# A fused attention and sparse-FFN kernel: the attention's output projection as three fp16 products instead of one fp32 product

## The reference

```
a = x
q, k, v = x@Wq, x@Wk, x@Wv          # 16 heads of 32
q, k = rotary(q), rotary(k)
attn = lightning_attn(q, k, v)      # linear attention in chunks of 128 tokens, a state carried from chunk to chunk
attn = attn * rsqrt(mean(attn^2) + 1e-5) * rms_w
attention_out = attn @ Wo           # <- the product that the change rewrites
z   = layernorm(x) @ ternary(W_syn).T + b_syn      # 2048 values per token
h   = z where z is among the top 204 of its token and positive, else 0
y   = h @ ternary(W_out).T + b_out
out = x-side terms + attention_out + layernorm(y-side)*gamma + beta
```

## Time and profile before

| what | value |
|---|---|
| median of 3 runs | 1044.32 us (1043.78 to 1046.3) |
| the profiled execution, its own time | 1045.96 us |
| its span, first to last instruction | 1044.0 us |
| mean granted TensorE clock | 0.973 |
| busy: PE, DVE, POOL, ACT | 971.1, 760.7, 694.9, 560.8 us |
| busy, PE, from 157.4 to 951.9 us | 794.5 of 794.5 us |

### The profile page before, as it was taken

The page is one execution under the profiler, slowest core; times in us unless marked ns, Lnnn a source line. Parts: engine busy times, 40 slices in busy tenths (PEclk is TensorE's granted clock), DMA queues, the critical chain, the costliest instruction groups (busy, mean ns, idle before and its releaser), DMA issues.

```text
span 1044.0 us, 18566 instructions
## 1 busy us (share of the span) xinstructions
PE 971.1 (93%) x6608; PEld 493.5 (47%) x6608; DVE 760.7 (73%) x2153; ACT 560.8 (54%) x715; POOL 694.9 (67%) x617
## 2 busy tenths in 40 slices
PE   1767799999999999999999999999999999999875
PEld 0333455554555555554555555554555555554432
DVE  2577767777877777777877777777877777776762
ACT  3877664654454665654455655654455655654421
POOL 1334777777778777777778777777777777777522
PEclk9978899999999999999999999999999999999976
DMA  9785756546455456545654555455554455555322
GB/s 295 258 201 91 145 88 112 101 92 112 100 103 96 83 96 112 97 97 111 97 107 78 96 101 111 92 101 111 93 111 89 81 104 110 89 106 101 72 51 60
DMA packets 328782, 113.65 MB, mean 109 GB/s; under 512 B 314736, under 2 KB 314992, under 8 KB 327792
## 3 DMA queue, kind: packets, MB, share of 16 engines
q1 hardware_dynamic: 326576, 108.25, 53.5%
q10 hardware_dynamic: 2112, 4.19, 1.3%
HBM read 25.38 MB, written 8.39 MB: 32 GB/s over the span
## 4 chain that ended last, share of the span: by engine, by line
PE 84%; DVE 1%; DMA 1%; issue 0%; POOL 0%; ACT 0%; SPq 0%; POOLq 0%; DVEq 0%
PE proj L735 42%; PE p_ffn L828 22%; PE p_wo L864 10%; PE p_av L803 3%; PE sbank L794 3%; PE p_av L849 2%; PE sbank L743 1%; PE sbank L885 1%; DMA area<-hl 1%; DVE area L1136 0%; PE sbank L897 0%; ACT hl L475 0%; PE p_wo L814 0%; POOL c L636 0%; SPq L299 0%
## 5 line engine op out<-in xcount | busy, mean ns | idle before, releaser
L735 PE MATMUL proj<-wqkv,xT 128*128 128x512 f16 x1152 | 257.6, 383 | 0.7 <-DVE wqkv L967 0.4
L735 PE MATMUL proj<-wsynT,xT 128*128 128x512 f16 x1024 | 246.2, 384 | 1.4 <-DVE area L1022 0.9
L828 PE MATMUL p_ffn<-woutT,area 128*128 128x512 f16 x1024 | 235.6, 385 | 10.9 <-DMA area<-hl 10.9
L735 PEld LDWEIGHTS proj<-wqkv,xT 128*128 128x128 f16 x1152 | 113.2, 99 | 131.7 <-issue 4.0
L468 ACT ACTIVATE Pr<-area,c 128x2048 f16<-128x2048 f32 x32 | 64.1, 2003 | 199.0 <-DVE c L1130 193.4
L828 PEld LDWEIGHTS p_ffn<-woutT,area 128*128 128x128 f16 x1024 | 101.9, 104 | 121.6 <-DMA area<-hl 11.1
L735 PEld LDWEIGHTS proj<-wsynT,xT 128*128 128x128 f16 x1024 | 93.2, 99 | 126.1 <-issue 35.0
L1022 DVE SCALAR_TENSOR_TENSOR area<-proj,c,gb 128x512 f32<-128x512 f32 x128 | 95.3, 745 | 42.8 <-PE proj L735 40.0
L631 POOL TENSOR_TENSOR hl<-area,hl 128x2048 f16<-128x2048 f32 x30 | 122.4, 4079 | 4.3 <-ACT hl L475 4.3
L864 PE MATMUL p_wo<-wo,pair_a 128*128 128x512 f32 x256 | 118.7, 607 | 0.0
L550 POOL TENSOR_TENSOR xhl<-xn,xhl 128x512 f16<-128x512 f32 x32 | 78.3, 2448 | 53.9 <-ACT xhl L397 53.9
(11 more groups left out here) (176 smaller groups left out, 1459.2 us busy)
## 6 DMA issues: line engine op xcount, KB each, us to landing
xr<-in_L_attn_x_dram SPq DMA_DIRECT2D x32, 256.0 KB, 3.2
out_dram<-pair_b SPq DMA_DIRECT2D x32, 256.0 KB, 2.1
area<-in_L_ffn_W_out_dram SPq DMA_DIRECT2D x3, 1024.0 KB, 6.0
woutT<-in_L_ffn_W_syn_dram ACTq DMA_DIRECT2D x2, 1024.0 KB, 13.2
area<-in_L_ffn_W_syn_dram ACTq DMA_DIRECT2D x2, 1024.0 KB, 17.7
woutT<-in_L_ffn_W_out_dram SPq DMA_DIRECT2D x2, 1024.0 KB, 6.5
area<-in_L_attn_Wq_dram SPq DMA_DIRECT2D x1, 1024.0 KB, 6.6
area<-in_L_attn_Wk_dram SPq DMA_DIRECT2D x1, 1024.0 KB, 9.7
```

The costliest lines, as they stand in the source:

```text
L735: last = nc.tensor.matmul(bank, xT[:, b.par, k, :], w, start=m == 0, stop=m == len(pairs) - 1)
L828: last = nc.tensor.matmul(p_ffn, hT[:, k, :], woutT[:, k % NB, :], start=k == 0, stop=k == 2 * NB - 1)
```

## The change

The Wo product becomes three fp16 products accumulated in one bank: high x high, high x low, low x high; twelve passes. The operands need a scale. Wo is multiplied by `rms_w`, its largest row sum is found as for the other weights, and it is scaled and split in the prologue. The attention output is multiplied, per token, by the power of two in `rstdR` (its exponent bits) times 256; the rest of `rstdR` (its mantissa) and the scale of Wo are put on at L1083. Since `aT` holds a token in a column, the powers have to be spread over the partitions: DVE puts them on a diagonal in bf16, and PE multiplies a tile of ones by it. The new names are `step_up`, `mant`, `diag`, `att_factor`, `ahl` (the halves).

The core of the diff:

```diff
-        wo = sb("wo", [P, KB, E], F32)
+        wo = sb("wo", [P, 2, KB, E], F16)
+        wo_in = masked.rearrange("p (b n) -> p b n", b=KB)
@@ SP, prologue
                 sp.wait_ge(S["syn_loaded3"], 16)
+                load_wo()
                 load(out_in[0], wt[:, 0, :], "out_loaded0")
                 load(dmask, t_dmask, "dmask_loaded")
-                load_wo()
@@ ACT, prologue, after qkv_out(second, 1)
+                act.wait_ge(S["wo_factor"], 1)
+                nc.scalar.activation(wo[:, 0], wo_in, ACT.Copy, scale=pc[:, 58:59]).then_inc(S["wo_high"], 1)
@@ ACT, step, between the second count (L483) and normalised(a)
+                wait(act, "an_ready", u, 1, 1)
+                wait(act, "wo_done", u, 1, 0)
+                nc.scalar.activation(ahl[:, 0], aT, ACT.Copy).then_inc(S["ah_ready"], 1)
@@ POOL, step, between the low half of h (L631) and low_half(a) (L550)
+                    wait(pool, "ah_ready", u, 1, 1)
+                    nc.gpsimd.tensor_tensor(ahl[:, 1], aT, ahl[:, 0], ALU.subtract).then_inc(S["al_ready"], 1)
@@ PE, prologue
                 projection(second, 1)
+                row_flipped(4)
+                row_spread(4)
                 projection(second, 2)
@@ PE, failures()
-                    nc.tensor.matmul(p_wo[:, 0:1], ones, fail, start=True, stop=True)
+                    nc.tensor.matmul(p_wo[0:1, 0:1], fail, ones[:, 0:1], start=True, stop=True)
@@ PE, step, after projection(b, 0)
+                    wait(pe, "diag_ready", u, 1, 1)
+                    nc.tensor.matmul(p_wo[:, P:2 * P], ones16, diag, start=True, stop=True)
@@ PE, step, the product
-                    wait(pe, "aT_ready", u, 1, 1)
-                    wait(pe, "fail_count", u, 1, 1)
-                    for g in range(HG):
-                        last = nc.tensor.matmul(p_wo, aT[:, g, :], wo[:, g, :], start=g == 0, stop=g == HG - 1)
+                    wait(pe, "ah_ready", u, 1, 1)
+                    terms = [(l, w, g) for l, w in ((0, 0), (0, 1), (1, 0)) for g in range(HG)]
+                    for m, (l, w, g) in enumerate(terms):
+                        if l and g == 0:
+                            wait(pe, "al_ready", u, 1, 1)
+                        last = nc.tensor.matmul(p_wo, ahl[:, l, g, :], wo[:, w, g, :], ...)
@@ DVE, prologue, after the bias sums, before syn_weights()
+                dve.wait_ge(S["wo_loaded"], 2 * 16)
+                for k in range(KB):
+                    last = nc.vector.tensor_scalar(wo_in[:, k, :], wo_in[:, k, :], rmsw[:, k:k + 1], None, ALU.mult)
+                last.then_inc(S["wo_scaled"], 1)
+                dve.wait_ge(S["wo_scaled"], 1)
+                nc.vector.reduce_sum(pc[:, 57:58], wo_in.rearrange("p b n -> p (b n)"), AX.X,
+                                     apply_absolute_value=True).then_inc(S["wo_abs"], 1)
+                row_topped(4)
+                dve.wait_ge(S["row_all"], 5)
+                then(nc.vector.tensor_scalar(pc[:, 59:60], p_ffn[:, 0:1], 1e-30, None, ALU.max))
+                pow2(pc[:, 60:61], pc[:, 59:60])
+                then(nc.vector.reciprocal(pc[:, 58:59], pc[:, 60:61]))
+                then(nc.vector.tensor_scalar(wo_back, pc[:, 60:61], 1.0 / (AS * WS), None, ALU.mult))
+                nc.vector.tensor_scalar(pc[:, 58:59], pc[:, 58:59], WS, None, ALU.mult).then_inc(S["wo_factor"], 1)
@@ DVE, prologue's end
+                nc.vector.scalar_tensor_tensor(wo[:, 1], wo_in, pc[:, 58:59], wo[:, 0], ALU.mult, ALU.subtract)
@@ DVE, step: factors(u), between the next guess (L1130) and masked (L1136)
+                    wait(dve, "rstdR_ready", u, 1, 1)
+                    nc.vector.tensor_scalar(step_up.bitcast(I32), rstdR.bitcast(I32), 0x7F800000, ...)
+                    nc.vector.tensor_scalar(mant.bitcast(I32), rstdR.bitcast(I32), 0x007FFFFF, 0x3F800000, ...)
+                    nc.vector.tensor_scalar(diag, ident, step_up, None, ALU.mult).then_inc(S["diag_ready"], 1)
+                    nc.vector.tensor_scalar(att_factor, mant, wo_back, None, ALU.mult)
@@ DVE, step: attention_normalised(u), after y and its statistics (L1166), before L1170
+                    wait(dve, "factors_spread", u, 1, 1)
+                    wait(dve, "aT_ready", u, 1, 1)
+                    spread = p_wo[:, P:2 * P].unsqueeze(1).to_broadcast([P, HG, P])
+                    nc.vector.scalar_tensor_tensor(aT, spread, AS, aT, ALU.mult, ALU.mult).then_inc(S["an_ready"], 1)
```

More of the change, by code:

```diff
@@ L37 @@
 WS = 2.0 ** 14
+AS = 256.0
 QS = 32.0
@@ L483, in step @@
                     nc.scalar.activation(unused, z[:, t.par, :], ACT.Sign, bias=nt1, accum_out=s2).then_inc(S["sum2"], 1)
+                if u:
+                    attention_high(u)
                 if a:
@@ L1058, in prologue @@
                                                ALU.add).then_inc(S["guess_ready"], 1)
-                dve.wait_ge(S["wo_loaded"], 2 * 16)
-                for k in range(KB):
-                    last = nc.vector.tensor_scalar(wo[:, k, :], wo[:, k, :], rmsw[:, k:k + 1], None, ALU.mult)
-                last.then_inc(S["wo_scaled"], 1)
+                dve.wait_ge(S["wo_high"], 1)
+                dve.wait_ge(S["wo_factor"], 1)
+                nc.vector.scalar_tensor_tensor(wo[:, 1], wo_in, pc[:, 58:59], wo[:, 0], ALU.mult,
+                                               ALU.subtract).then_inc(S["wo_low"], 1)
             def step(dve, i, p):
@@ L1081, in attention_added, with factors, attention_normalised @@
                     wait(dve, "beta_added", u, 1, 1)
+                    wait(dve, "factor_step", u, 3, 3)
+                    nc.vector.scalar_tensor_tensor(slot(xr, u), p_wo, att_factor, slot(xr, u), ALU.mult,
+                                                   ALU.add).then_inc(S["att_added"], 1)
+                def factors(u):
                     wait(dve, "rstdR_ready", u, 1, 1)
[L1083 to L1084 removed]
+                    nc.vector.tensor_scalar(step_up.bitcast(I32), rstdR.bitcast(I32), 0x7F800000, None,
+                                            ALU.bitwise_and).then_inc(S["factor_step"], 1)
+                    nc.vector.tensor_scalar(mant.bitcast(I32), rstdR.bitcast(I32), 0x007FFFFF, 0x3F800000, ALU.bitwise_and,
+                                            ALU.bitwise_or).then_inc(S["factor_step"], 1)
+                    wait(dve, "factor_step", u, 3, 1)
+                    nc.vector.tensor_scalar(diag, ident, step_up, None, ALU.mult).then_inc(S["diag_ready"], 1)
+                    wait(dve, "factor_step", u, 3, 2)
+                    nc.vector.tensor_scalar(att_factor, mant, wo_back, None, ALU.mult).then_inc(S["factor_step"], 1)
+                def attention_normalised(u):
+                    wait(dve, "factors_spread", u, 1, 1)
+                    wait(dve, "aT_ready", u, 1, 1)
+                    spread = p_wo[:, P:2 * P].unsqueeze(1).to_broadcast([P, HG, P])
+                    nc.vector.scalar_tensor_tensor(aT, spread, AS, aT, ALU.mult, ALU.mult).then_inc(S["an_ready"], 1)
                 def segments(k):
@@ L1166, in step @@
                     nc.vector.bn_stats(st6[:, 1, :], y).then_inc(S["yst"], 1)
+                if u:
+                    attention_normalised(u)
                 if t:
```

59 lines of the change are left out of this document (40 added, 19 removed).

## The result

The changed kernel took 1065.34 us (median of 4 runs, 1063.01 to 1068.48), and the kernel before 1044.05 beside it (4 runs, 1043.77 to 1046.3): a ratio of 1.0201, with a 95% interval from 1.0171 to 1.0231. It is slower by about 2%, and outside the predicted range (1026 to 1052). The profiled execution took 1065.79 us with a span of 1064.0, which is 20.0 more than before; its mean granted clock is 0.966 (0.973 before).

The account below looks back on a forecast made before the run. The prediction took TensorE's unbroken run of 29 steps of 29.43 us as the bound. Prologue +3.2, steps -9.6 and end +2.4 gave -4.0 us: 1040.0, or 1040.3 on the median, range 1026 to 1052.

Parts of the forecast that it names:

- The spreading product: PE, each step: one added bf16 pass of 128 columns, put at 0.08 us.
- The four operations of `factors`: DVE, ahead of `masked`: three one-column operations and a 128x128 one, put at 0.42 us, bounds 0.3 and 0.9.
- hold: DVE's L1186 (L1267 after the change) kept back by POOL's new low half, 0.95 us, bounds 0.5 and 1.2.
- The power for `rD`: POOL's L636, behind L550: 0.95 us late, with everything behind it on POOL.
- The wait for PE ahead of the first z chunk: DVE's 1.14 us idle time in each step, forecast to be gone.
- The end: Behind 981.39 us, where PE is not the bound: 2.4 us added, bounds 1 and 3.5.
- PE's own step: PE's work per step, forecast as 29.43 - 0.90 - 0.05 + 0.08 = 28.56 us.
- rival 4: `factors` on DVE's loop take 0.9 instead of 0.42, second count 0.5 later, step 29.6, kernel 1055 us; chance 0.15.
- What is late next: POOL's lateness followed to probabilities and sums of squares: loop 29.05, step taken as 29.1 us, 9.6 off over 29 steps.
- the term of 3.2 us: The prologue and second step, up to 127.87 us: 3.2 us added.
- first piece: Prologue: Wo lands at 39, scaling takes 1.89, PE waits 1.2 us; syn sums 2.2 us later, bounds 0.8 and 5.
- second piece: Second step: ACT's `attention_high` ahead of the signs that the last W_out transposes wait for, 0.55 us more.

Follow-up runs that it names:

- one more POOL operation: The kernel before with a 128x512 subtraction of constants added on POOL in each step, where the low half would go: 1045.61 us, 1.0004.
- POOL order run: The changed kernel with POOL's low halves of q and k ahead of the output sum, which waits for DVE's failure flag: 1047.85 us, 1.0017.
- late operation in the kernel before: The kernel before plus a 128x512 POOL subtraction per step that also waits for ACT's normalised x: 1049.61 us, 1.0031.

## Why the prediction was wrong

**What was right.** The row of L864 became 2.59 us of L904, as worked out. The spreading product takes 0.06 us of PE's step (0.08 predicted). The four operations of `factors` fill 0.50 us, from 620.35 to L1215 at 620.85 (0.42). POOL's operation goes first and L1267 takes 3.19 us (3.3), a hold of 0.84 (0.95). The power for `rD` is 1.05 us later behind the count (0.95). The wait for PE ahead of the first z chunk is gone. Ahead of L937 PE's weight load waits 0.68 us a step for POOL's sums of squares and PE itself 0.19, which lie side by side and don't add up (about 0.5 predicted); the piece of the chain is 0.38 us, where it was 0.12 (0.34). The end took 2.1 us more (2.4). The failure count did not get cheaper: 0.12 as before, 0.05 predicted off, and the half of the W_out product behind it takes 3.56 us in the chains of four of the kernels above, where it took 3.48. Why was not tried. With this PE's own step is 29.43 - 0.90 + 0.06 + 0.08 = 28.67 (28.56).

The size of the hold came out better than its reasoning. I scaled 0.23 us of an operation of 0.40 by the columns. What three rows have in common is another rule: DVE loses what is left of POOL's operation less 0.2 us. It lost 0.84 of 1.04 here, 0.22 of 0.43 beside the one more POOL operation, and 0.23 of 0.42 in the earlier trace rows.

One size was off without deciding anything. From the count read to `masked` it takes 2.52 us in the median step, where it took 1.49: besides `factors`, the branch lets DVE go on 0.42 us later (1.51 behind the read, 1.09 before). What the branch does there I did not test. `masked` itself takes 2.34 in every step, where it took 2.54 to 2.57 in 20 of 32, so its end comes 0.8 later. ACT hides most of it, as predicted, though not all: the second guess step L1254 comes 10.63 us behind the read, 10.44 before. So 0.19 arrive where I had 0.05, far from the 0.5 of rival 4.

**What failed in the steady part** is the step "What is late next", which gave 29.05 and 29.1 us for a step that measured 29.63. I followed POOL's 0.95 us of lateness by two ways, to the probabilities and to the sums of squares, and stopped there. A third way goes on over POOL's last operation, the low halves of q and k, to the end of DVE's top-k. I had said that POOL's work and two-operand DVE work add up, and applied it to L1186 only. The kernel before had the rows for it: L578 ends at 600.63, the selection starts at 600.68. The DVE loop, 28.9 in the prediction, plus 0.77 for the held flag, plus the 0.14 more of `factors` and less the 0.11 by which the hold was shorter, is 29.7, and 29.63 was measured; this sum was made afterwards and takes the flag's price for every step, though in half of them it was the selection, and those steps were longer (29.85 against 29.52). The POOL order run shows this cause alone, in size (0.67 us a step, 19.4 us over 29 steps), and the late operation in the kernel before shows it from the other side. And neither hold is dear alone: 28.96 with that of L1267, 28.84 with those of the top-k, 29.63 with both kinds.

With the meeting gone the step is 28.96, against 29.1 predicted. That part of the argument, a POOL–PE loop somewhat longer than PE's step, was right in its mechanism: moving the sums of squares took the wait away, and the step fell to 28.85. But it holds the step only 0.11 us above what is left without it, not the 0.54 between 28.56 and 29.1.

**What failed in the start** is the term of 3.2 us, of which 12.0 were measured. Its first piece (+2.2 for the syn sums, 6.4 measured) had Wo landing too late, at 39, and took 1.89 us for its scaling from a row with only 0.40 us of POOL work beside it; it took 4.85. The wait of PE that came of it, put at 1.2 us, was 3.91 (and 5.2 or 5.3 in the five other kernels with this prologue), and it cost a second time: the 12 passes behind it ran at a granted clock of 0.53 and took 2.36 us more. With 1.25 for the new products, and PE at this place 1.16 earlier than before, these are the 6.4. Moving the wait away took back 4.9 us in the traces. That the scaling is long because of POOL was not tried by itself, though the ends of the four blocks, each 0.27 to 0.29 us behind a POOL operation, point to it. The section of the Trainium skill named above says that a DVE operation in a two-port mode excludes GpSimd's as one with two SBUF inputs does; no run here shows in which mode the scaling ran. The second piece, the second step, was put at 0.55 us for ACT's new copy. The place that mattered was PE's product that waits for DVE's diagonal, with 24 passes, a copy of ACT and a sign queued behind it; I had checked that wait only in a step of the loop, where DVE is early. It too cost the clock besides the wait (11.15 us for 36 passes that took 9.62). Moving it gave back 3.8 of the 5.9.

In the sum: -9.6 + 0.67 x 29 = +9.8 by the meeting, less 0.14 x 29 = 4.1 by which the rest of the step was better than forecast, is the +5.7 of the steady part (5.9 measured). The three steps in it (29.1 forecast, 28.96 and 29.63 measured) make this come out by themselves; what stands on its own is the 0.67. Of the 24.0 us between forecast and result, 15.5 are the steady part, 8.8 the start and -0.3 the end.

## What to carry to other kernels

When an engine gets late, follow its lateness to the last instruction of its step, and look at what each of its operations will run beside from then on, not only at who waits for it. A near miss in the trace, such as 0.05 us between the end of a POOL operation and the start of a two-operand DVE one, is a cost that waits. And a new wait in a long in-order stream must be checked in the first steps too, where the engine that feeds it is busy with the prologue's work: each of the two here cost some 4 to 5 us once, by the wait and by a lower granted clock behind it.

## What the runs showed of the hardware

- An operation of DVE with two SBUF tensors is held to the end of the POOL operation that it meets, however small it is: 0.15 became 0.92 us, 0.25 became 1.26, for one and 32 columns. Two POOL operations back to back (L599 x2) hold it over what is left of both. With a per-partition scalar as the second operand the flag took 0.20 at the same place.
- Who goes first is settled within 0.1 us: POOL, 0.12 ahead, held DVE for 0.84 and stayed at 1.16; POOL, 0.08 behind, took 3.17 and DVE stayed at 2.35. At 0.02 behind POOL still went first.
- A held DVE operation of 128x2048 lost 0.2 us less than what was left of POOL's: 0.84 of 1.04, 0.22 of 0.43, 0.23 of 0.42.
- Scaling four 128x512 blocks of fp32 took 4.85 and 4.97 us beside POOL's additions (in the first, each block ended 0.27 to 0.29 us behind one of them), and 1.89 with only 0.40 us of POOL work beside it.
- After PE had waited 3.91 us, 12 passes took 4.95 us at a granted clock of 0.53, against 2.59 at 1.00; after 2.98 us, 24 passes took 6.70 at 0.77, against 5.18.
